# A factorization-machine kernel: one-hot gates from a key in PSUM, picked values kept in PSUM, and a new order for the last jobs

## The chip, the cores and the metric

The kernel runs on one core of one Trainium2 chip. The metric is the device time of one execution in microseconds, the median of several. Engines are named as the profile does: PE is TensorE's matmul side and PEld its weight loads, DVE is VectorE, ACT ScalarE, POOL GpSimd, and SP the engine that issues most transfers.

## The reference

2048 samples, each with 13 dense values and 26 category numbers. Every category field has a table of 12,500 rows of 32 embedding values and one linear value.

```python
sp_emb = emb_tables[fidx, sp_input]          # 2048 x 26 x 32
lin_vals = lin_tables[fidx, sp_input, 0]
lin_output = ds_input @ lin_w.T + lin_b + jnp.sum(lin_vals, axis=1, keepdims=True)
s = jnp.sum(sp_emb, axis=1)
bi_pooled = 0.5 * (s * s - jnp.sum(sp_emb * sp_emb, axis=1))
x = jnp.concatenate([bi_pooled, ds_input], axis=1)
h = jax.nn.relu(x @ w1.T + b1)               # 45 -> 256
h = jax.nn.relu(h @ w2.T + b2)               # 256 -> 128
out = jax.nn.sigmoid(h @ fw.T + fb + lin_output)
```

So the kernel needs, for each sample, the sum and the sum of squares of 26 looked-up rows of 33 values, and then three small layers.

## The kernel before

The lookups are split between two ways of fetching a row.

**19 fields by gather.** The samples form 16 tiles of 128. For each tile, POOL issues 19 indirect DMAs (line 248), one for each field, that bring 128 rows of 33 values into one of three `rows` buffers (`RING = 3`). A tile's first gather waits until the tile three before it has been reduced. DVE sums the rows (`g_sum`, line 314), ACT squares them (line 460), and DVE sums the squares (`g_sq`, line 317).

**7 fields by matmul.** The samples form 4 blocks of 512; a job is one field and one block, 28 jobs in all. A table of 12,500 categories is laid out as 128 partitions x 9 chunks x 11 sub-rows. For each chunk there is a gate, a 128x512 tile with a one where the sample's category lies in this partition and chunk. PE multiplies the chunk's table piece (122 columns for each of three value groups, as a high and a low part) with the gate and adds up over the chunks in `cand`, three PSUM banks of 122x512; two `cand` tiles alternate. This is 9 x 6 = 54 matmuls a job (line 550). The 122 columns hold the 11 possible sub-rows, so DVE's `pick` (line 298) keeps the right one by a compare with the sample's sub-row code and writes it to `picked` in SBUF. DVE adds `picked` to `acc` (line 303), ACT squares `picked` in place (line 455), and DVE adds that to `sq_acc` (line 310).

**The gates.** Three code rows per job come broadcast from DRAM (`codes`). DVE's `make_where` (line 272) makes a mask that holds a chunk value where the partition fits. Three gates are made by DVE from that mask (line 281, two SBUF tensor inputs `where` and `all_one`), six by ACT from it (lines 423, 434, 426). There are 16 gate slots.

**The tables.** A field's table is loaded to `stage` and split by ACT into `high` (line 413) and by DVE into `low` (line 288), in three pieces of three chunks each. `CASTS` says after which job. For the last field, number 6, pieces 0 and 1 are made in iteration 20 and piece 2 in iteration 21, and PE needs piece 2 at chunk 6 of job 22.

**The order.** Each engine has a list of its own. Its main loop runs over j = 0..27. In iteration j, DVE makes the gates of job j+1, picks job j, makes the mask of j+2, casts `low` pieces (`CASTS`), sums a gathered tile (`TILE_AT`: tiles 0 to 11 at the even j from 2 to 24, tiles 12, 13 and 14 at j = 25, 26, 27) and adds the squares. PE runs the 54 matmuls of job j once `cand` is free.

**The end.** Blocks 0, 1 and 2 are complete after jobs 22, 23 and 25, block 3 after job 27. For each block PE folds `acc`, `sq_acc` and the tile sums into two PSUM banks (`fold_block`, lines 554 to 572: sums to `bank_a`, squares to `bank_b`), ACT and DVE form x (lines 469, 470, 325), and PE, ACT run the layers. For blocks 0 to 2 the fold stands after job 23, 24 or 26 and the layers lie between chunks of the next job. Tile 15 arrives last; block 3 is therefore done in two parts, samples 0 to 383 and the last 128. In the prediction E(j) is the moment at which PE ends job j.

## Time and profile before

| | |
|---|---|
| median of 3 runs | 465.53 us (461.74 to 466.88) |
| profiled execution | 466.34 us, its span 464.5 us |
| PE busy | 418.8 us (90%) |
| POOL busy | 357.2 us (77%) |
| DVE busy | 278.0 us (60%) |
| ACT busy | 263.4 us (57%) |

The span runs from the first to the last instruction of the trace; the execution's time is 1.8 us longer. Busy shares are averages over two stages: the jobs up to 20, and the end with folds and layers. PE's busy time is modelled for pipelined matmuls, so 90% does not say how fast they follow one another; the start times do.

### The profile page before, as it was taken

The page shows a single profiled execution, that of the slowest core. Times are in us where ns is not written, and L with a number is a line of the kernel's source. Part 1 is how long each engine was busy: PE and PEld are TensorE (multiplying, and loading weights), DVE is VectorE, ACT ScalarE, POOL GpSimd, SP SyncE. Part 2 cuts the span into 40 slices and gives each one's busy share as a digit, 9 for nine tenths or more (in the row PEclk, how much of TensorE's full clock was granted, in tenths as well). Part 3 has the DMA queues.
Part 4 walks back from the last instruction along what each step waited for, and adds up shares of the span by engine and source line. Part 5 has one row for each costly group of instructions (what it writes and reads, how often), then busy time and mean ns, then how long its engine had stood idle before and what let it go on. Part 6 is the DMA issues. An engine that isn't in the chain of part 4 may idle for free.

```text
span 464.5 us, 4661 instructions
## 1 busy us (share of the span) xinstructions
PE 418.8 (90%) x1700; PEld 302.6 (65%) x1700; DVE 278.0 (60%) x283; ACT 263.4 (57%) x378; POOL 357.2 (77%) x312
## 2 busy tenths in 40 slices
PE   0499999999999999999999999699999999877564
PEld 0377777777777777777777777477564666543122
DVE  6524463687959786878778795776815438122320
ACT  3457776567666776777666676673663717211121
POOL 5777777787878887877777887777877777777770
PEclk9999999999999999999999999889999999959787
DMA  7543336323362326334643325234324222222220
GB/s 208 126 144 50 48 48 185 54 44 45 47 187 28 38 33 192 43 45 48 181 56 47 46 51 184 13 48 46 42 13 47 12 15 11 12 14 14 11 14 3
DMA packets 23600, 28.94 MB, mean 62 GB/s; under 512 B 6245, under 2 KB 22407, under 8 KB 22794
## 3 DMA queue, kind: packets, MB, share of 16 engines
q0 software_dynamic: 9728, 5.16, 19.1%
q1 hardware_dynamic: 13848, 23.49, 17.1%
q8 instruction: 13, 0.21, 0.2%
q14 instruction: 11, 0.08, 0.1%
HBM read 28.53 MB, written 0.09 MB: 62 GB/s over the span
## 4 chain that ended last, share of the span: by engine, by line
POOL 75%; issue 22%; DMA 1%; PE 1%; POOLq 0%; ACT 0%; DVE 0%
POOL rows L248 75%; DMA rows<-table,row_idx 1%; DMA idx_raw<-sparse 1%; PE bank_b L563 0%; POOLq L83 0%; PE bank_a L571 0%; PE cand L587 0%; PE bank_b L571 0%; ACT stage L476 0%; PE cand L580 0%; PE cand L595 0%; DVE g_sum L314 0%; ACT stage L481 0%; DVE xT L325 0%; ACT stage L469 0%
## 5 line engine op out<-in xcount | busy, mean ns | idle before, releaser
L248 POOL DMA_INDIRECT rows<-table,row_idx x304 | 356.4, 1172 | 95.5 <-issue 92.3
L550 PE MATMUL cand<-gates,high 128*122 128x512 f32 x756 | 304.6, 403 | 22.2 <-DVE gates L281 18.2
L550 PE MATMUL cand<-gates,low 128*122 128x512 f32 x756 | 301.3, 399 | 0.0
L550 PEld LDWEIGHTS cand<-gates,high 128*122 128x122 f32 x756 | 140.8, 186 | 68.4 <-DVE gates L281 18.2
L550 PEld LDWEIGHTS cand<-gates,low 128*122 128x122 f32 x756 | 140.6, 186 | 37.4 <-issue 0.7
L455 ACT ACTIVATE picked<-picked 122x1536 f32<-122x1536 f32 x24 | 35.7, 1487 | 96.8 <-DVE acc L303 96.8
L298 DVE SCALAR_TENSOR_TENSOR picked<-codes,sub_id,cand 122x1536 f32<-122x1536 bf16 x24 | 43.5, 1812 | 75.1 <-PE cand L550 75.1
L434 ACT ACTIVATE distance<-where,bias 128x512 bf16<-128x512 bf16 x112 | 71.4, 708 | 6.4 <-DVE where L272 6.2
L426 ACT ACTIVATE gates<-distance,bias 128x512 fp32r<-128x512 bf16 x112 | 71.4, 709 | 0.0
L281 DVE SCALAR_TENSOR_TENSOR gates<-where,all_one 128x512 fp32r<-128x512 bf16 x84 | 53.5, 692 | 0.9 <-ACT sq_acc L452 0.9
L288 DVE TENSOR_TENSOR low<-stage,high 128x1098 fp32r<-128x1098 f32 x21 | 27.2, 1302 | 32.1 <-ACT high L413 32.1
L310 DVE TENSOR_TENSOR sq_acc<-sq_acc,picked 122x1536 f32<-122x1536 f32 x24 | 42.1, 1753 | 4.5 <-ACT picked L455 4.5
L303 DVE TENSOR_TENSOR acc<-acc,picked 122x1536 f32<-122x1536 f32 x24 | 42.4, 1765 | 0.8
L423 ACT ACTIVATE gates<-where,bias 128x512 fp32r<-128x512 bf16 x56 | 37.0, 709 | 0.0
L314 DVE TENSOR_REDUCE g_sum<-rows 128x33 f32<-128x627 f32 (+2 forms) x17 | 21.2, 1249 | 25.3 <-DMA rows<-table,row_idx 25.3
L413 ACT CAST high<-stage 128x1098 fp32r<-128x1098 f32 x21 | 22.9, 1097 | 6.0 <-DMA stage<-tabs 4.2
L272 DVE SCALAR_TENSOR_TENSOR where<-codes,part_id 128x512 bf16<-128x512 bf16 x28 | 20.9, 748 | 5.7 <-DMA codes<-codes_dram 5.7
L460 ACT ACTIVATE squares<-rows 128x608 f32<-128x608 f32 (+2 forms) x17 | 11.5, 674 | 19.6 <-DMA rows<-table,row_idx 19.6
L317 DVE TENSOR_REDUCE g_sq<-squares 128x32 f32<-128x608 f32 (+2 forms) x17 | 20.0, 1175 | 1.5 <-ACT squares L460 1.5
L557 PE MATMUL bank_a<-acc,fold 122*33 122x512 f32 (+2 forms) x30 | 12.9, 572 | 8.7 <-DVE sq_acc L310 8.7
L298 DVE SCALAR_TENSOR_TENSOR acc<-codes,sub_id,cand 122x1536 f32<-122x1536 bf16 x4 | 7.3, 1816 | 20.8 <-PE cand L550 20.8
L452 ACT ACTIVATE sq_acc<-acc 122x1536 f32<-122x1536 f32 x4 | 6.0, 1488 | 15.6 <-DVE acc L298 15.6
(70 smaller groups left out, 102.3 us busy)
## 6 DMA issues: line engine op xcount, KB each, us to landing
codes<-codes_dram SPq DMA_DIRECT2D x28, 384.0 KB, 4.8
stage<-tabs SPq DMA_DIRECT2D x6, 1647.0 KB, 10.1
rows<-table,row_idx POOLq DMA_INDIRECT x304, 3.3
stage<-tabs SPq DMA_DIRECT2D x3, 549.0 KB, 5.4
idx_raw<-sparse SPq DMA_DIRECT2D x1, 208.0 KB, 2.5
w_sb<-w2t SPq DMA_DIRECT2D x1, 128.0 KB
xT<-dense_rows SPq DMA_DIRECT2D x1, 120.0 KB
codes_dram<-col_code SPq DMA_DIRECT2D x1, 84.0 KB
```

The costliest lines, as they stand in the source:

```text
L248: pool.indirect_dma_start(out=rows[t % RING][:, g * W:(g + 1) * W], out_offset=None, in_=table[:, :], in_offset=bass.IndirectOffsetOnAxis( ...
L281: nc.vector.scalar_tensor_tensor(gates[:, g % SLOTS, :], where[j % 2][:, :], float(VALUE[ORDER[k]]), all_one[:, :], ALU.is_equal, ALU.mult ...
L288: nc.vector.tensor_tensor(low[f % 2][:, c, :, :].rearrange("p c q m -> p (c q m)"), stage[:, s], high[f % 2][:, c, :, :].rearrange("p c q ...
L298: nc.vector.scalar_tensor_tensor(into, codes[j % 3][0:M, SUB, :].unsqueeze(1).broadcast_to([M, PARTS, N]), sub_id[0:M, 0:1], cand[j % 2][0 ...
L303: nc.vector.tensor_tensor(acc[:, b, :, :], acc[:, b, :, :], picked[:, :, :], ALU.add).then_inc(summed, 1)
L310: nc.vector.tensor_tensor(sq_acc[:, b, :, :], sq_acc[:, b, :, :], picked[:, :, :], ALU.add).then_inc(sq_summed, 1)
L413: nc.scalar.copy(high[f % 2][:, c, :, :].rearrange("p c q m -> p (c q m)"), stage[:, s]).then_inc(high_made, 1)
L423: nc.scalar.activation(slot, where[j % 2][:, :], ACT.Relu, bias=bias[:, k:k + 1], scale=1.0 if ORDER[DVE_GATES + k] == 8 else -1.0).then_i ...
L426: nc.scalar.activation(slot, distance[:, k - ENDS, :], ACT.Relu, bias=bias[:, ACT_GATES:ACT_GATES + 1], scale=-1.0).then_inc(act_gates, 1)
L434: nc.scalar.activation(distance[:, k, :], where[j % 2][:, :], ACT.Square, bias=bias[:, ENDS + k:ENDS + k + 1]).then_inc(distance_made, 1)
L455: nc.scalar.activation(picked[:, :, :], picked[:, :, :], ACT.Square).then_inc(picked_squared, 1)
L550: last = nc.tensor.matmul(cand[j % 2][0:M, q, :], part[f % 2][:, k, q, :], gates[:, g % SLOTS, :], start=(k == 0 and s == 0), stop=(k == C ...
```

## The change

**Codes.** A sample now has one key per field, chunk x 128 + partition, and the sub-row code; both travel as fp16, so two rows are broadcast in place of three. ACT copies a job's key row into the PSUM bank `bank_a` (`copy_keys`). DVE makes five gates (before: three), each by one `tensor_scalar` that compares `bank_a` with a per-partition number; `where` and `all_one` are gone. ACT makes four gates (before: six) by Square and Relu on the key row in SBUF. There are 18 gate slots, and the gates of job j+2 are made in iteration j (before: j+1).

**Picks.** `pick` writes its result over `cand` in PSUM (the four jobs of field 0 still write `acc`), the two additions read it there, and ACT squares it there. `cand` is therefore released to PE by the addition of squares (`sq_summed`), two jobs ahead, and no longer by the pick.

**Order.** `bank_a` is taken by the keys, so for blocks 0 to 2 the fold of sums, the fold of squares, both halves of layer 1, layer 2 and layer 3 go one after another through `bank_b`. The table `STEPS` puts each after a chunk of jobs 24 to 27.

```diff
-    SLOTS = 16
+    SLOTS = 18
-    DVE_GATES = 3
+    DVE_GATES = 5
-    FOLD_AFTER = {FULL + 3: 0, FULL + 4: 1, FULL + 6: 2}
-    LAYERS_IN = {FULL + 4: 0, FULL + 5: 1, FULL + 7: 2}
+    J0 = FULL + 4
+    STEPS = {(J0, 0): (0, F1), (J0, 4): (0, F2), (J0, 7): (0, L1A), (J0 + 1, 0): (0, L1B), (J0 + 1, 2): (0, L2),
...
+            pool.iota(key_i[:, 0, :], pattern=[[P, CHUNKS]], base=0, channel_multiplier=1).then_inc(made_ids, 1)
+            pool.iota(key_i[:, 1, :], pattern=[[-P, CHUNKS]], base=0, channel_multiplier=-1).then_inc(made_ids, 1)
...
-            def make_where(j):
-
-                dve.wait_ge(codes_in[j % 3], 16 * (j // 3 + 1))
-                if j >= 2:
-                    dve.wait_ge(act_gates, (j - 1) * ACT_GATES)
-                nc.vector.scalar_tensor_tensor(where[j % 2][:, :], codes[j % 3][:, LO, :], part_id[:, 0:1],
-                                               codes[j % 3][:, VAL, :], ALU.is_equal, ALU.mult).then_inc(where_made, 1)
...
-                    nc.vector.scalar_tensor_tensor(gates[:, g % SLOTS, :], where[j % 2][:, :], float(VALUE[ORDER[k]]),
-                                                   all_one[:, :], ALU.is_equal, ALU.mult).then_inc(dve_gates, 1)
+                    nc.vector.tensor_scalar(gates[:, g % SLOTS, :], bank_a[:, :], key_of[:, k:k + 1], None,
+                                            ALU.is_equal).then_inc(dve_gates, 1)
...
-                into = acc[:, b, :, :] if f == 0 else picked[:, :, :]
+                into = acc[:, b, :, :] if f == 0 else cand[j % 2][0:M, :, :]
...
-                    nc.vector.tensor_tensor(acc[:, b, :, :], acc[:, b, :, :], picked[:, :, :],
+                    nc.vector.tensor_tensor(acc[:, b, :, :], acc[:, b, :, :], cand[j % 2][0:M, :, :],
...
-                    nc.vector.tensor_tensor(sq_acc[:, b, :, :], sq_acc[:, b, :, :], picked[:, :, :],
+                    nc.vector.tensor_tensor(sq_acc[:, b, :, :], sq_acc[:, b, :, :], cand[j % 2][0:M, :, :],
...
             for j in range(NJ):
-                if j + 1 < NJ:
-                    make_gates(j + 1)
                 pick(j)
+                if j in (J0 + 1, J0 + 2):
+                    make_x(j - J0)
                 if j + 2 < NJ:
-                    make_where(j + 2)
+                    make_gates(j + 2, 0, 2)
+                add_squares(j)
+                if j + 2 < NJ:
+                    make_gates(j + 2, 2, DVE_GATES)
                 for f, g in CASTS.get(j, ()):
                     low_piece(f, g)
+                if j == J0 - 1:
+                    make_x(0)
                 if j in TILE_AT:
...
+            def copy_keys(j):
+
+                act.wait_ge(codes_in[j % 3], 16 * (j // 3 + 1))
                 if j >= 1:
-                    act.wait_ge(act_gates, j * ACT_GATES)
+                    act.wait_ge(dve_gates, j * DVE_GATES)
+                nc.scalar.copy(bank_a[:, :], codes[j % 3][:, KEY, :]).then_inc(key_copied, 1)
...
+                if j + 2 < NJ:
+                    copy_keys(j + 2)
+                    make_gates(j + 2, 0, FIRST_ACT)
+                if j == J0:
+                    relu1(0, 1)
                 square_picked(j)
...
+                if j + 2 < NJ:
+                    make_gates(j + 2, FIRST_ACT, ACT_GATES)
                 for f, g in CASTS.get(j, ()):
...
+            def fold_sq(m, tiles):
                 b, w = BLOCK[m], COLS[m]
+                if m < BLOCKS:
+
+                    pe.wait_ge(lin_copied, m + 1)
                     pe.wait_ge(y_made, m)
...
             for j in range(NJ):
-                if j >= 2:
-                    pe.wait_ge(cand_free, j - 1)
+                if 2 <= j < BLOCKS + 2:
+                    pe.wait_ge(picked, j - 1)
+                elif j >= BLOCKS + 2:
+
+                    pe.wait_ge(sq_summed, j - 1 - BLOCKS)
```

The instruction order of DVE around the pick of job 20, before (`picked` is the SBUF tile, L288 the `low` pieces, L314 and L317 the tile sums):

```order
L281 SCALAR_TENSOR_TENSOR gates<-where,all_one 128x512 [waits gates_used,where_made]
L281 SCALAR_TENSOR_TENSOR gates<-where,all_one 128x512 [waits gates_used] x2
L298 SCALAR_TENSOR_TENSOR picked<-codes,sub_id,cand 122x1536 [waits sq_summed,gates_used]
L303 TENSOR_TENSOR acc<-acc,picked 122x1536 [waits cand_free]
L272 SCALAR_TENSOR_TENSOR where<-codes,part_id 128x512 [waits act_gates,codes_in1]
L288 TENSOR_TENSOR low<-stage,high 128x1098 [waits high_made] x2
L314 TENSOR_REDUCE g_sum<-rows 128x33 [waits gathered0]
L317 TENSOR_REDUCE g_sq<-squares 128x32 [waits squared]
L310 TENSOR_TENSOR sq_acc<-sq_acc,picked 122x1536 [waits picked_squared]
```

and the same place now:

```order
L293 SCALAR_TENSOR_TENSOR cand<-codes,sub_id,cand 122x1536 [waits gates_used]
L298 TENSOR_TENSOR acc<-acc,cand 122x1536 [waits picked]
L278 TENSOR_SCALAR gates<-bank_a,key_of 128x512 [waits gates_used,key_copied]
L278 TENSOR_SCALAR gates<-bank_a,key_of 128x512 [waits gates_used]
L305 TENSOR_TENSOR sq_acc<-sq_acc,cand 122x1536 [waits picked_squared]
L278 TENSOR_SCALAR gates<-bank_a,key_of 128x512 [waits gates_used,key_copied]
L278 TENSOR_SCALAR gates<-bank_a,key_of 128x512 [waits gates_used] x2
L285 TENSOR_TENSOR low<-stage,high 128x1098 [waits high_made] x2
L309 TENSOR_REDUCE g_sum<-rows 128x33 [waits gathered0]
L312 TENSOR_REDUCE g_sq<-squares 128x32 [waits squared]
```

The gates moved from in front of the pick to behind it, and they now belong to job j+2; the addition of squares moved up, ahead of the casts and the tile sums.

ACT in iteration 21, up to the last `high` piece of field 6, before:

```order
L423 ACTIVATE gates<-where,bias 128x512 [waits gates_used] x2
L426 ACTIVATE gates<-distance,bias 128x512 [waits gates_used,distance_made]
L426 ACTIVATE gates<-distance,bias 128x512 [waits gates_used] x3
L455 ACTIVATE picked<-picked 122x1536 [waits summed]
L413 CAST high<-stage 128x1098
```

and now (L436 squares the pick, L403 is the `high` piece):

```order
L436 ACTIVATE cand<-cand 122x1536 [waits summed]
L418 ACTIVATE distance<-codes,minus_key 128x512 [waits act_gates]
L418 ACTIVATE distance<-codes,minus_key 128x512
L425 ACTIVATE gates<-distance,one 128x512 [waits gates_used,distance_made]
L425 ACTIVATE gates<-distance,one 128x512 [waits gates_used]
L403 CAST high<-stage 128x1098
```

Two distances and two gates of job 23 now stand between the square and the `high` piece, which stood directly behind it.

PE behind the last gate matmul of job 27, before:

```order
L557 MATMUL bank_a<-acc,fold 33x384 [waits sq_summed]
L557 MATMUL bank_a<-acc,fold 33x384 x2
L571 MATMUL bank_a<-ident,g_sum 33x128 [waits reduced]
L571 MATMUL bank_a<-ident,g_sum 33x128 x2
L563 MATMUL bank_b<-sq_acc,fold 32x384 [waits y_made]
```

and now:

```order
L604 MATMUL bank_b<-xT,wl_sb 1x512 [waits h2_made]
L605 MATMUL bank_b<-stage,fw_sb 1x512
L560 MATMUL bank_a<-acc,fold 33x384 [waits summed]
L560 MATMUL bank_a<-acc,fold 33x384 x2
L579 MATMUL bank_a<-ident,g_sum 33x128 [waits reduced]
L579 MATMUL bank_a<-ident,g_sum 33x128 x2
L571 MATMUL bank_b<-sq_acc,fold 32x384 [waits y_made,lin_copied,sq_summed]
```

Layer 3 of block 2 stands behind the job, and the fold of squares of block 3 waits for `lin_copied`, which ACT sets after it has read the folded sums.

## Rows read from the trace of the kernel before

**Rows 1.** The page, chain of work that ended last, shares by engine.

```profile
POOL 75%; issue 22%; DMA 1%; PE 1%; POOLq 0%; ACT 0%; DVE 0%
```

**Rows 2.** One line's instructions (L248): ns min/median/max, first and last start.

```profile
L248 POOL DMA_INDIRECT rows<-table,row_idx x304: 940/944/4380, 4.8 to 452.6; - x152
```

**Rows 3.** Timeline, POOL: start us, us, engine, line, operation [idle before].

```profile
92.69 4.37 POOL L248 DMA_INDIRECT rows<-table,row_idx  x1 [0.30 <-issue]
97.37 0.94 POOL L248 DMA_INDIRECT rows<-table,row_idx  x1 [0.30 <-issue]
98.61 1.96 POOL L248 DMA_INDIRECT rows<-table,row_idx  x1 [0.30 <-issue]
```

**Rows 4.** Timeline, DVE, the same stretch.

```profile
92.67 1.76 DVE L310 TENSOR_TENSOR sq_acc<-sq_acc,picked 122x1536 f32<-122x1536 f32 x1
94.34 1.91 DVE L281 SCALAR_TENSOR_TENSOR gates<-where,all_one 128x512 fp32r<-128x512 bf16 x3
96.15 1.82 DVE L298 SCALAR_TENSOR_TENSOR picked<-codes,sub_id,cand 122x1536 f32<-122x1536 bf16 x1
98.00 1.76 DVE L303 TENSOR_TENSOR acc<-acc,picked 122x1536 f32<-122x1536 f32 x1
```

**Rows 5.** Groups of instructions by form: xcount | busy us, mean ns | idle before.

```profile
L434 ACT ACTIVATE distance<-where,bias 128x512 bf16<-128x512 bf16 x112 | 71.4, 708 | 6.4 <-DVE where L272 6.2
L455 ACT ACTIVATE picked<-picked 122x1536 f32<-122x1536 f32 x24 | 35.7, 1487 | 96.8 <-DVE acc L303 96.8
L288 DVE TENSOR_TENSOR low<-stage,high 128x1098 fp32r<-128x1098 f32 x21 | 27.2, 1302 | 32.1 <-ACT high L413 32.1
L413 ACT CAST high<-stage 128x1098 fp32r<-128x1098 f32 x21 | 22.9, 1097 | 6.0 <-DMA stage<-tabs 4.2 <-DVE sub_id L367 1.9
L314 DVE TENSOR_REDUCE g_sum<-rows 128x33 f32<-128x627 f32 x15 | 19.8, 1321 | 14.9 <-DMA rows<-table,row_idx 14.9
L317 DVE TENSOR_REDUCE g_sq<-squares 128x32 f32<-128x608 f32 x15 | 18.7, 1244 | 1.5 <-ACT squares L460 1.5
L325 DVE TENSOR_TENSOR xT<-stage,bank_b 32x512 f32<-32x512 f32 x3 | 2.0, 670 | 0.6 <-ACT stage L469 0.6
```

**Rows 6.** Waits: us in total, times, longest us.

```profile
DVE g_sum L314 <- DMA rows<-table,row_idx: 25.3, 5, 9.4
```

**Rows 7.** Timeline, DVE, the picks of jobs 16, 20, 23 and 24.

```profile
233.60 1.81 DVE L298 SCALAR_TENSOR_TENSOR picked<-codes,sub_id,cand 122x1536 f32<-122x1536 bf16 x1 [2.97 <-PE cand L550]
283.86 1.81 DVE L298 SCALAR_TENSOR_TENSOR picked<-codes,sub_id,cand 122x1536 f32<-122x1536 bf16 x1 [3.07 <-PE cand L550]
328.22 1.81 DVE L298 SCALAR_TENSOR_TENSOR picked<-codes,sub_id,cand 122x1536 f32<-122x1536 bf16 x1
353.77 1.81 DVE L298 SCALAR_TENSOR_TENSOR picked<-codes,sub_id,cand 122x1536 f32<-122x1536 bf16 x1 [15.54 <-PE cand L550]
```

**Rows 8.** Timeline, PE: the end of a stop, and two passes of layer 1.

```profile
300.31 0.76 PE L550 MATMUL cand<-gates,high 128*122 128x512 f32 x1 [3.99 <-issue]
...
340.81 1.12 PE L580 MATMUL bank_a<-xT,w_sb 48*128 48x512 f32 x2
341.77 1.02 PE L580 MATMUL bank_b<-xT,w_sb 48*128 48x512 f32 x2
```

**Rows 9.** Windows: each engine's busy us (instructions), PEclk, DMA share, GB/s.

```profile
302.00:305.00 3.00, 3.00 (x8) 2.27 (x8) 2.96 (x3) 0.38 (x1) 2.39 (x3) 0.50 0.28 38
```

**Rows 10.** Timeline, the end: DVE, PE, ACT, DVE.

```profile
426.66 1.81 DVE L298 SCALAR_TENSOR_TENSOR picked<-codes,sub_id,cand 122x1536 f32<-122x1536 bf16 x1 [17.00 <-PE cand L550]
435.30 2.13 PE L557 MATMUL bank_a<-acc,fold 122*33 122x384 f32 x3 [8.68 <-DVE sq_acc L310]
450.31 0.48 ACT L487 ACTIVATE y<-cand 1x384 f32<-1x384 f32 x1 [0.99 <-PE cand L595]
455.82 0.38 DVE L314 TENSOR_REDUCE g_sum<-rows 128x33 f32<-128x132 f32 x1 [3.32 <-DMA rows<-table,row_idx]
```

More of the change, by code:

```diff
@@ L142, in build_deep_fm @@
         bank_b = pb("bank_b", [P, N])
-        TAIL = (cand[0][:, 0, :], cand[0][:, 1, :], cand[0][:, 2, :], cand[1][:, 0, :])
-        H1A, H1B, H2P, YP = ([pick] * 3 + [tail] * 2 for pick, tail in zip((bank_a, bank_b, bank_a, bank_b), TAIL))
+        SUM_BANK = [bank_b] * 3 + [bank_a] * 2
+        H1A, H1B, H2P, YP = ([bank_b] * 3 + [cand[k][:, q, :]] * 2 for k, q in ((0, 0), (0, 1), (0, 2), (1, 0)))
         idx_in = sem("idx_in")
@@ L454, in square_picked @@
                     act.wait_ge(summed, j + 1 - BLOCKS)
-                    nc.scalar.activation(picked[:, :, :], picked[:, :, :], ACT.Square).then_inc(picked_squared, 1)
+                    nc.scalar.activation(cand[j % 2][0:M, :, :], cand[j % 2][0:M, :, :], ACT.Square).then_inc(picked_squared, 1)
             def square_rows(t, at, f0, f1):
@@ L517, in _ @@
                     high_piece(f, g)
+                if j == J0:
+                    sigmoid(0)
+                if j == J0 + 1:
+                    relu1(1, 1)
+                    relu2(1)
+                if j == J0 + 2:
+                    relu1(2, 0)
+                    relu1(2, 1)
                 if j in TILE_AT:
@@ L552, in chunk, with fold_sum @@
                 last.then_inc(gates_used, 1)
-            def fold_block(m, tiles):
-                b, w = BLOCK[m], COLS[m]
-                for q in range(PARTS):
-                    nc.tensor.matmul(bank_a[0:W, w], fold[0:M, q, :], acc[:, b, q, w], start=(q == 0), stop=False)
-                pe.wait_ge(reduced, 2 * (tiles[-1] + 1) - 1)
-                fold_tiles(bank_a, g_sum, W, tiles).then_inc(folded, 1)
-                if 1 <= m < BLOCKS:
+            def fold_sum(m, tiles):
+                b, w, bank = BLOCK[m], COLS[m], SUM_BANK[m]
+                for q in range(PARTS):
+                    nc.tensor.matmul(bank[0:W, w], fold[0:M, q, :], acc[:, b, q, w], start=(q == 0), stop=False)
+                pe.wait_ge(reduced, 2 * (tiles[-1] + 1) - 1)
+                fold_tiles(bank, g_sum, W, tiles).then_inc(folded, 1)
+            def fold_sq(m, tiles):
+                b, w = BLOCK[m], COLS[m]
+                if m < BLOCKS:
+                    pe.wait_ge(lin_copied, m + 1)
                     pe.wait_ge(y_made, m)
@@ L573, in fold_tiles, with layer1 @@
                 return last
-            def layer1(m):
+            def layer1(m, k):
                 w = COLS[m]
                 c = slice(BLOCK[m] * N + w.start, BLOCK[m] * N + w.stop)
-                pe.wait_ge(x_made, 2 * m + 2)
-                for k, bank in enumerate((H1A[m], H1B[m])):
-                    nc.tensor.matmul(bank[:, w], w1_sb[:, k * P:(k + 1) * P], xT[:, c], start=True,
-                                     stop=True).then_inc(h1_done, 1)
+                pe.wait_ge(lin_copied, m + 1)
+                pe.wait_ge(x_made, m + 1)
+                if k == 1 and m < BLOCKS - 1:
+                    pe.wait_ge(h1_made, m * HC + 1)
+                nc.tensor.matmul((H1A, H1B)[k][m][:, w], w1_sb[:, k * P:(k + 1) * P], xT[:, c], start=True,
+                                 stop=True).then_inc(h1_done, 1)
             def layer2(m):
```

232 lines of the change are left out of this document (114 added, 118 removed).

## The prediction

> **What bounds the kernel now.** I read the chain of work that ended last first. It is POOL and POOL's own issue time for 97% of the span [rows 1]: nothing released POOL but its previous gather. All 304 gathers run without a break from 4.8 to 452.6 us [rows 2]. Half of them take 0.944 us or less, one takes 4.38. With the 0.30 us in front of each [rows 3], an undisturbed gather is worth 1.245 us, so 304 would last 378.5 us. They last 452.6 + 0.9 - 4.8 = 448.7 us. Some 70 us are prolongations.
>
> The timelines of POOL and DVE beside each other say what prolongs them [rows 3, 4]. The gather at 98.61 ends 1.02 us later than a plain one would; it began while `acc` was being added (98.00 to 99.76). The gather at 92.69 is 3.43 us too long: the addition of squares and three gates follow one another from 92.67 to 96.25. But the gather at 97.37 is a plain 0.94 although it lies within the pick of 96.15 to 97.97. What differs is the operands: the additions, gates and `low` pieces read two SBUF tensors, the pick reads one from SBUF and one from PSUM. So DVE instructions with two SBUF tensor inputs hold gathers up, and one with a PSUM input does not.
>
> PE is the second bound, close behind. Up to job 20 it sets the pace: DVE waits for PE at the picks of jobs 16 and 20, 50.26 us apart, 12.57 us a job [rows 7]. From there on the late gathers stop DVE, five waits with 25.3 us in all [rows 6], and DVE's queue stops PE.
>
> **The change, part by part.**
>
> *Port.* The three large DVE operations and the gates get a PSUM input; the mask goes. Only the 21 `low` pieces of 1.30 us [rows 5] keep two SBUF inputs. They prolong gathers by nothing to 21 x 1.30 = 27 us; I take half, since they would catch a gather at a random point. POOL alone would be through at 4.8 + 378.5 + 14 = 397 us. The bound then passes to PE.
>
> *DVE's load per job.* Pick 1.81 and two additions of 1.76 with one PSUM operand, for which the pick is the nearest row (1.82 against 1.76) [rows 4]: 3 x 1.82 = 5.5. Five gates with PSUM input: nearest above is a 512-wide operation with a PSUM operand, 0.67 [rows 5], below the present gates, 1.91/3 = 0.64 [rows 4]; I take 0.67, 3.3 in all. `Low` pieces three jobs in four (1.0), a tile every second job (2.57/2 = 1.3) [rows 5]. Sum 11.1 of 12.57 us: hidden behind PE with 1.5 us to spare. ACT has 8 gate operations of at most 0.71, the square 1.49, the `high` pieces 0.8 and 0.6 for the keys, under 9 us: hidden too.
>
> *The new wait.* PE may write `cand` again only after pick 1.8, addition 1.8, ACT's square 1.5 and the addition of squares 1.8, 6.9 us after E(j) [rows 4, 5]. PE needs it 12.57 us after E(j), since the other `cand` is in use meanwhile. Cost nothing; the cover is 5.7 us. Queued behind this addition are three gates of job j+2, which PE needs only in the job after next.
>
> *The last table piece.* Here the new order costs. Piece 2 of field 6 is cast in iteration 21 and PE wants it at chunk 6 of job 22, E(21) + 6/9 x 12.57 = 8.4 us. Before, ACT's `high` stood directly behind the square. Iteration 20 on DVE, counted from E(20): pick and addition 3.6, two gates 1.3, the addition of squares until 6.9, three gates until 8.9, two `low` pieces until 11.5, tile sums until 14.0. So the pick of job 21 is 1.4 late. Then on ACT: the square until 6.5, four gate operations until 9.1, `high` until 10.2 and DVE's `low` until 11.5 after E(21). PE stops 3.1 us. In the trace a stop of 3.99 us [rows 8] was followed by a stretch at half clock (0.50, the lower of the two levels; 3 us and 8 matmuls in [rows 9]). Six such microseconds cost 3; I take 1.2 here, between none and 3, as this stop is shorter. Together 4.3 us.
>
> *Folds and layers.* Before, job 24 with one block's fold and layers took 353.77 - 328.22 = 25.6 us, so a block costs 13.0 us of PE [rows 7]. The matmuls are the same, in other places. I followed each wait: x of block 0 stands on DVE in iteration 23 and waits for a fold about 14 us after E(23), but the next pick comes only at 20.7. ACT's Relus find their inputs. Nothing stops PE by more than a few tenths. The three blocks cost 39 us as before, of which layer 3 of block 2 (two passes of 0.96 [rows 8], 1.9) now lies behind job 27.
>
> *Ring.* POOL now waits for its buffers: tile 14 for iteration 24, tile 15 for iteration 25. By the queues this last one is free about 62 us after E(23), at 387, and tile 15 is in `rows` at 414. DVE reaches it at about 425. So the gathers are off the path altogether.
>
> *Start.* The code chain is two operations shorter and a third fewer code bytes travel; ACT's copy of 0.6 replaces the mask. Between nothing and 1 us gained; I take nothing.
>
> *End.* Before, the first part of block 3 took from the last pick, 426.66, to its y at 450.79, 24.1 us [rows 10]. Now PE's fold of sums waits for tile 14's sum only, 8.2 us after the pick (8.64 before [rows 10]); its `acc` passes are done by then; ACT's reading (1.0) lies between the folds in place of 0.5 behind them. From fold to fold's end I get 4.8 us for 7.2, so 20.8 us in all. For the last 128 samples the gathers set the time before: from 455.82 [rows 10] to the end, 464.5, 8.7 us. Now ACT's squares and DVE's sums of tile 15 stand behind y of the first part (1.9 us), then 8.7. Sum from the last pick 31.4 us.
>
> **The sum.** E(20) = 283.8 as before [rows 7]. Jobs 21 to 27: 7 x 12.57 = 88.0. Stop at job 22: 4.3. Folds and layers 39.0, less 1.9 for layer 3 of block 2 and 1.9 for its layer 2, which comes behind chunk 8, so that the pick does not wait for it: 35.2. The last pick starts at 411.3, and with 31.4 the span ends at 442.7. The execution is 1.8 longer than its span: 444.5 against 466.3 profiled. The median shown is 0.8 below the profiled run, which gives **443.5 us**. Its own range is 435 (no stop, the start and additions better) to 453 (a second stop with half clock, DVE 0.2 us a job over its room).
>
> **The rivals.**
>
> *A, the lock stays (0.07).* If gathers are also held up by additions with one SBUF operand, or by the gates' writes, POOL ends near 450 as now and the time is 465.5. Against it: the gather within the pick [rows 3, 4]. For it: no row shows a `tensor_scalar` that reads PSUM. There the Trainium skill, "VectorE: DVE Perf Modes", section "Why PSUM operands drop a tier", says that PSUM has one read port for DVE, so a PSUM operand excludes the mode that takes both SBUF ports; by it this rival falls, and no run here shows it yet.
>
> *B, DVE becomes the bound (0.06), slower.* Three large operations and the gates read PSUM, and the pick and ACT's square write it in place, which no row shows. The PSUM work is 8.8 us a job, the room 1.5. At 1.17 times the price DVE sets the pace; slower than before needs 22 us more, 0.8 a job, so 1.26 times. At 1.3 times it is 28 x (2.6 - 1.5) = 31 us, 474 us. For it speaks that there is little room and no slack in iterations with casts and sums; against it the pick, 0.05 above an SBUF operation. The Trainium skill, "VectorE: DVE Perf Modes", section on the TRN2 errata, gives 120 fixed cycles with a PSUM source against 58 from SBUF; by that estimate each operation costs 0.06 us more, half a microsecond a job, and the sum stays.
>
> *C, PE stops again and again at the end (0.08).* Each of the 17 steps between chunks of jobs 24 to 27 waits for ACT or DVE, whose queues hold gates in front of the Relus. Four stops of about 1.5 us and half clock behind two of them add 12 us: 456. Still faster.
>
> **Chances.** The forecast has 0.79. A measurement of this kernel tells about 1% (4.7 us) from no change. Faster by more: the forecast and C, 0.87. Within 1%: A, 0.07. Slower: B, 0.06. The range of 8 in 10 is 435 to 457; it takes in C and leaves out A and B.
>
> **What would show it.** Gathers of 0.94 us throughout, those at `low` pieces excepted, and POOL with waits for `reduced` behind tile 12. Picks 12.57 us apart with DVE waiting for PE. A stop of PE of about 3 us at chunk 6 of job 22. No DVE wait for gathers. The chain of waits on PE instead of POOL. It is wrong if the additions in PSUM last over 2.1 us, if prolonged gathers remain beside them, or if E(27) - E(23) is above 89 us.

## The result, and the profile after

The changed kernel takes 442.88 us (median of 4 runs, 442.65 to 444.62), the kernel before on the same chip 466.2 (median of 4 runs). The ratio is 0.9538 (95% interval 0.9464 to 0.9613): 4.6% faster. The forecast was 443.5 us in a range of 435 to 457. One of the four runs of the kernel before took 612.89 us; it is left out of the ratio.

That holds for this chip. On another chip the same changed kernel is 17% slower than the kernel before; the experiments below show on what this hangs.

The page of the changed kernel: the shares of busy time, the chain of work that ended last by engine, the costliest groups (count | busy us, mean ns | idle before and what ended it), and the DMA queues (packets, MB, share).

```profile
span 441.3 us, 4680 instructions
PE 410.7 (93%) x1700; PEld 297.4 (67%) x1700; DVE 300.6 (68%) x303; ACT 249.6 (57%) x350; POOL 292.4 (66%) x314
PE 87%; DVE 7%; DMA 3%; ACT 2%; issue 1%; DVEq 0%; ACTq 0%
L253 POOL DMA_INDIRECT rows<-table,row_idx x304 | 291.3, 958 | 116.8 <-issue 90.8
L278 DVE TENSOR_SCALAR gates<-bank_a,key_of 128x512 fp32r<-128x512 f32 x140 | 96.8, 742 | 7.3 <-ACT bank_a L411 6.3
L298 DVE TENSOR_TENSOR acc<-acc,cand 122x1536 f32<-122x1536 f32 x24 | 42.1, 1753 | 0.8
q8 instruction: 13, 0.21, 0.2%
```

The chain is PE's now; before it was POOL's [rows 1]. PE is released by itself at nearly every step.

The gathers answer to [rows 2]: their last start moved from 452.6 to 409.1.

```profile
L253 POOL DMA_INDIRECT rows<-table,row_idx x304: 939/944/1901, 4.9 to 409.1; - x152
```

POOL's timeline while DVE works without a pause, and DVE's beside it. They answer to [rows 3] and [rows 4]; the columns are start, us, engine, line, operation, idle before.

```profile
259.54 0.94 POOL L253 DMA_INDIRECT rows<-table,row_idx  x1 [0.30 <-issue]
...
263.29 0.94 POOL L253 DMA_INDIRECT rows<-table,row_idx  x1 [0.31 <-issue]
```

```profile
257.07 1.82 DVE L293 SCALAR_TENSOR_TENSOR cand<-codes,sub_id,cand 122x1536 f32<-122x1536 f16 x1 [2.42 <-PE cand L553]
258.93 1.75 DVE L298 TENSOR_TENSOR acc<-acc,cand 122x1536 f32<-122x1536 f32 x1
260.60 1.40 DVE L278 TENSOR_SCALAR gates<-bank_a,key_of 128x512 fp32r<-128x512 f32 x2
262.18 1.75 DVE L305 TENSOR_TENSOR sq_acc<-sq_acc,cand 122x1536 f32<-122x1536 f32 x1 [0.18 <-ACT cand L436]
...
282.07 1.82 DVE L293 SCALAR_TENSOR_TENSOR cand<-codes,sub_id,cand 122x1536 f32<-122x1536 f16 x1 [3.69 <-PE cand L553]
295.70 1.82 DVE L293 SCALAR_TENSOR_TENSOR cand<-codes,sub_id,cand 122x1536 f32<-122x1536 f16 x1
304.45 1.29 DVE L285 TENSOR_TENSOR low<-stage,high 128x1098 fp32r<-128x1098 f32 x1
310.36 1.82 DVE L293 SCALAR_TENSOR_TENSOR cand<-codes,sub_id,cand 122x1536 f32<-122x1536 f16 x1 [4.61 <-PE cand L553]
...
410.66 1.82 DVE L293 SCALAR_TENSOR_TENSOR cand<-codes,sub_id,cand 122x1536 f32<-122x1536 f16 x1 [0.47 <-PE cand L553]
```

The gathers at 259.54 and 263.29 start while an addition runs (258.93 and 262.18) and take 0.94 us, as do those beside the pick and the gates. Only 14 of the 304 gathers take more than 0.96 us; 12 of them start beside a `low` piece, which still has two SBUF inputs.

The stop of PE in job 22, against [rows 8], and the granted clock around it, against [rows 9] (PE, PEld, DVE, ACT, POOL busy, PEclk, DMA share, GB/s):

```profile
305.89 0.46 PE L553 MATMUL cand<-gates,high 128*122 128x512 f32 x1 [2.97 <-DVE low L285]
```

```profile
303.00:306.00 3.00, 0.11 (x1) 0.14 (x2) 2.75 (x4) 2.75 (x5) 2.39 (x3) 1.00 0.30 14
306.00:308.00 2.00, 2.00 (x9) 1.61 (x10) 0.00 (x0) 1.65 (x3) 1.51 (x2) 1.00 0.24 21
```

The stop is where the prediction put it, released by `low`, and 2.97 us long. The clock stayed at its higher level (1.00); behind the 3.99 us stop of before it was 0.50.

The longest waits (us in total, times, longest):

```profile
DVE cand L293 <- PE cand L553: 51.5, 15, 7.1
POOL rows L253 <- DVE g_sq L312: 22.9, 5, 13.4
```

There is no wait of DVE for a gathered row, where [rows 6] had 25.3 us; POOL waits for its buffers instead, five times, in front of tiles 11 to 15.

### The profile page after: what moved, and what is told of

It reads as the page before. It is cut to its first block, busy times and chain, and to the rows that moved or that the text cites. A ratio compares the mean times of both kernels' runs of the same rounds, so it can differ in the third digit from the quotient of the medians.

```text
span 441.3 us, 4680 instructions
## 1 busy us (share of the span) xinstructions
PE 410.7 (93%) x1700; PEld 297.4 (67%) x1700; DVE 300.6 (68%) x303; ACT 249.6 (57%) x350; POOL 292.4 (66%) x314
## 4 chain that ended last, share of the span: by engine, by line
PE 87%; DVE 7%; DMA 3%; ACT 2%; issue 1%; DVEq 0%; ACTq 0%
PE cand L553 76%; PE bank_b L571 3%; PE bank_b L560 2%; PE bank_b L579 1%; PE bank_b L590 1%; DMA codes_dram<-col_code 1%; DVE cand L293 1%; DVE acc L298 1%; DVE gates L278 1%; ACT cand L436 1%; DVE low L285 1%; DMA codes<-codes_dram 1%; PE bank_b L597 1%; DVE g_sum L309 1%; DMA idx_raw<-sparse 1%
## 5 line engine op out<-in xcount | busy, mean ns | idle before, releaser
L253 POOL DMA_INDIRECT rows<-table,row_idx x304 | 291.3, 958 | 116.8 <-issue 90.8
L278 DVE TENSOR_SCALAR gates<-bank_a,key_of 128x512 fp32r<-128x512 f32 x140 | 96.8, 742 | 7.3 <-ACT bank_a L411 6.3
L436 ACT ACTIVATE cand<-cand 122x1536 f32<-122x1536 f32 x24 | 34.4, 1435 | 86.3 <-DVE acc L298 86.3
L293 DVE SCALAR_TENSOR_TENSOR cand<-codes,sub_id,cand 122x1536 f32<-122x1536 f16 x24 | 43.7, 1822 | 51.6 <-PE cand L553 51.5
L425 ACT ACTIVATE gates<-distance,one 128x512 fp32r<-128x512 bf16 x112 | 75.1, 716 | 3.1 <-PE cand L553 1.4
L418 ACT ACTIVATE distance<-codes,minus_key 128x512 bf16<-128x512 f16 x112 | 74.1, 711 | 0.1
L305 DVE TENSOR_TENSOR sq_acc<-sq_acc,cand 122x1536 f32<-122x1536 f32 x24 | 42.0, 1752 | 5.3 <-ACT cand L436 5.3
L298 DVE TENSOR_TENSOR acc<-acc,cand 122x1536 f32<-122x1536 f32 x24 | 42.1, 1753 | 0.8
L403 ACT CAST high<-stage 128x1098 fp32r<-128x1098 f32 x21 | 22.9, 1097 | 6.3 <-DMA stage<-tabs 6.3
L411 ACT CAST bank_a<-codes 128x512 f32<-128x512 f16 x28 | 16.3, 583 | 11.7 <-DVE gates L278 6.9
L571 PE MATMUL bank_b<-sq_acc,fold 122*32 122x512 f32 (+2 forms) x30 | 12.9, 574 | 1.1 <-issue 1.1
```

The costliest lines, as they stand in the source:

```text
L253: pool.indirect_dma_start(out=rows[t % RING][:, g * W:(g + 1) * W], out_offset=None, in_=table[:, :], in_offset=bass.IndirectOffsetOnAxis( ...
L278: nc.vector.tensor_scalar(gates[:, g % SLOTS, :], bank_a[:, :], key_of[:, k:k + 1], None, ALU.is_equal).then_inc(dve_gates, 1)
L293: nc.vector.scalar_tensor_tensor(into, codes[j % 3][0:M, SUB, :].unsqueeze(1).broadcast_to([M, PARTS, N]), sub_id[0:M, 0:1], cand[j % 2][0 ...
L298: nc.vector.tensor_tensor(acc[:, b, :, :], acc[:, b, :, :], cand[j % 2][0:M, :, :], ALU.add).then_inc(summed, 1)
L305: nc.vector.tensor_tensor(sq_acc[:, b, :, :], sq_acc[:, b, :, :], cand[j % 2][0:M, :, :], ALU.add).then_inc(sq_summed, 1)
L418: nc.scalar.activation(distance[:, k, :], codes[j % 3][:, KEY, :], ACT.Square, bias=minus_key[:, c:c + 1]).then_inc(distance_made, 1)
```

## The experiments

They ran on four other chips. There the kernel before takes 549 to 566 us by the medians (535 to 590 in single runs) in place of 465, so each run is compared with runs of the kernel before on its own chip, and its numbers stand apart from the result above. Ranges are given where no interval came with a run.

### Additions and gates from SBUF

The first two undo one part of the change each, to see which operands hold gathers. In e1 the picks go back to an SBUF tile:

```diff
+        picks = sb("picks", [M, PARTS, N])
-                into = acc[:, b, :, :] if f == 0 else cand[j % 2][0:M, :, :]
+                into = acc[:, b, :, :] if f == 0 else picks[:, :, :]
-                    nc.vector.tensor_tensor(acc[:, b, :, :], acc[:, b, :, :], cand[j % 2][0:M, :, :],
+                    nc.vector.tensor_tensor(acc[:, b, :, :], acc[:, b, :, :], picks[:, :, :],
...
```

> The changed kernel, but pick writes its result to a tile in SBUF again and both additions and ACT's square work there. Gates, order and PE's waits stay as changed. Theory (a DVE instruction with two SBUF tensor inputs holds gathers up): the 48 additions prolong gathers again, by about 1 us each. POOL's last gather ends near 430 us in place of 410, later gathers stop DVE at tiles 14 and 15, time about 448 us (444 to 455). Rival (the mask and the gates held the gathers up, not the additions): gathers stay at 0.94 us and the time at 443.

Measured: 558.2 us (541.2 to 573.8), before 564.3 (547.6 to 582.9). The groups of e1, and a stretch of its POOL and DVE timelines:

```profile
L254 POOL DMA_INDIRECT rows<-table,row_idx x304 | 333.7, 1098 | 201.6 <-DVE g_sq L315 106.0
L301 DVE TENSOR_TENSOR acc<-acc,picks 122x1536 f32<-122x1536 f32 x24 | 42.2, 1760 | 0.8
```

```profile
150.88 0.94 POOL L254 DMA_INDIRECT rows<-table,row_idx  x1 [16.91 <-DVE g_sq L315]
152.12 2.31 POOL L254 DMA_INDIRECT rows<-table,row_idx  x1 [0.30 <-issue]
154.74 0.94 POOL L254 DMA_INDIRECT rows<-table,row_idx  x1 [0.30 <-issue]
155.99 1.76 POOL L254 DMA_INDIRECT rows<-table,row_idx  x1 [0.30 <-issue]
```

```profile
151.86 1.76 DVE L301 TENSOR_TENSOR acc<-acc,picks 122x1536 f32<-122x1536 f32 x1
153.54 1.41 DVE L279 TENSOR_SCALAR gates<-bank_a,key_of 128x512 fp32r<-128x512 f32 x2
155.18 1.76 DVE L308 TENSOR_TENSOR sq_acc<-sq_acc,picks 122x1536 f32<-122x1536 f32 x1 [0.23 <-ACT picks L439]
```

The gathers that start while an addition runs (152.12 and 155.99) end 0.8 us behind the addition's end; the one that starts beside the gates (154.74) is plain, though an addition begins during it. So what counts is the DVE instruction that runs when a gather starts. All 38 gathers of e1 that start beside one of the 48 additions are prolonged: they take 1.36 to 2.52 us, 1.86 in the mean, or 34.8 us in all over the plain 0.944. The rest of the 42.4 us by which POOL is busier than in the changed kernel (333.7 against 291.3) falls mainly to the `low` pieces: 15 gathers start beside one, 11.4 us over the plain time, where the changed kernel has 3.9. The additions themselves last as long from SBUF (1760 ns) as with a PSUM operand (1753). This part of the mechanism is shown, by the gathers' own durations. Its worth in time is not: the kernel's time on this chip follows something else, as e2 shows. The Trainium skill, "SBUF — State Buffer", section "SBUF: two separate sides", tells of a port pair that DVE and GpSimd lock against each other, for a DVE operation with two SBUF inputs too, though there only against a GpSimd operation that reads SBUF; in the trace the gathers, whose row indices lie in SBUF, are held, by 0.92 us each in the mean (1.86 against 0.94).

e2 keeps the sums in PSUM and reads the keys from SBUF:

```diff
-                    nc.vector.tensor_scalar(gates[:, g % SLOTS, :], bank_a[:, :], key_of[:, k:k + 1], None,
+                    nc.vector.tensor_scalar(gates[:, g % SLOTS, :], keys[:, :], key_of[:, k:k + 1], None,
-                nc.scalar.copy(bank_a[:, :], codes[j % 3][:, KEY, :]).then_inc(key_copied, 1)
+                nc.scalar.copy(keys[:, :], codes[j % 3][:, KEY, :]).then_inc(key_copied, 1)
```

> The changed kernel, but ACT copies the keys to an fp32 tile in SBUF in place of the PSUM bank, and DVE's five gates read it there: one SBUF tensor input each. Theory in its narrow form (only two tensor inputs hold gathers): gathers stay at 0.94 us, gates last 0.64 to 0.74, time 443. Theory in its wide form (an fp32 tensor_scalar from SBUF also takes the second read port, and is faster for it): gates fall to 0.35 to 0.5 us, 140 of them prolong gathers by 0.1 to 0.3 us on average each, POOL's busy time rises by 15 to 40 us, and the time is 443 to 447, since POOL has room.

Measured: 638.1 us (633.0 to 640.4), ratio to before 1.1354 (1.1139 to 1.157).

```profile
L254 POOL DMA_INDIRECT rows<-table,row_idx x304 | 297.6, 979 | 289.7 <-DVE g_sq L313 196.1
L279 DVE TENSOR_SCALAR gates<-keys,key_of 128x512 fp32r<-128x512 f32 x140 | 61.1, 487 | 10.1 <-issue 7.5
```

A gather that is held, and the gates beside it:

```profile
268.38 1.24 POOL L254 DMA_INDIRECT rows<-table,row_idx  x1 [0.30 <-issue]
268.23 1.27 DVE L279 TENSOR_SCALAR gates<-keys,key_of 128x512 fp32r<-128x512 f32 x3
```

A gate from SBUF takes 487 ns in place of 742. These gates hold gathers too. Of the 23 gathers that start beside one, 20 take more than 0.96 us; the mean is 1.12 and the longest 1.29 us, and in the median they end 0.82 us behind that gate, just as gathers do behind an addition. Beside the gates from PSUM, 83 gathers of the changed kernel start and none is prolonged. The price is small, 4.0 us of POOL's 297.6, because the gates are short and few gathers meet one, not because they leave gathers free; the `low` pieces add 5.0 us here. The wide form of the expectation came true in its two mechanisms (0.35 to 0.5 us a gate, 0.1 to 0.3 us a gather), and missed the time. The Trainium skill, "VectorE: DVE Perf Modes", section "Why PSUM operands drop a tier", says that a PSUM operand shuts out the mode with both read ports; 742 against 487 ns agrees.

Against expectation was the time. e1, whose gathers are held up, is 80 us faster than e2, whose gathers are nearly free. Something in free gathers costs time on this chip. A window of e1, 160 us long (PE, PEld, DVE, ACT and POOL busy us with instructions, PEclk, DMA share, GB/s), has PE at its full rate with the gathers 1.5 us apart:

```profile
160.00:320.00 160.00, 156.65 (x670) 121.87 (x668) 128.86 (x118) 101.26 (x139) 127.53 (x107) 1.00 0.35 63
```

### Fewer gathers

Both kernels with 15 gathers a tile in place of 19 (four gathered fields are left out of the sums). The edit of e4, and with the old names of e3:

```diff
+    SKIP = 4
-                for g in range(GF):
+                for g in range(SKIP, GF):
-                    dve.wait_ge(gathered[t % RING], (t // RING + 1) * 16 * GF)
-                    sum_rows(t, t, 0, GF)
+                    dve.wait_ge(gathered[t % RING], (t // RING + 1) * 16 * (GF - SKIP))
+                    sum_rows(t, t, SKIP, GF)
...
```

> The kernel before with 15 gathers a tile in place of 19 (four of the 19 gathered fields are left out of the sums). Theory (all of the gain came from POOL's gathers leaving the path): POOL needs 449 x 15/19 = 354 us, is off the path, and the old kernel ends on PE: last pick at about 284 + 88 + 39 = 411 us, then 24 us to y of the first part and 10 for the last 128 samples, time about 447 us (443 to 451). Rival (the new gates and the new order of folds and layers gave part of it): 453 us or more.

> The changed kernel with 15 gathers a tile in place of 19 (the same four fields are left out). Theory (gathers are off the path now): 442 to 443 us, nothing gained beyond about 0.5 us of shorter sums. Rival (ring waits and late tiles still cost at the end): 438 us or less.

Measured: e3, the kernel before with 15, 476.5 us, ratio 0.8478 (0.8347 to 0.861). e4, the changed kernel with 15, 550.0 us, ratio 0.9765 (0.9419 to 1.0112). So the kernel before gains 88 us from 64 gathers fewer, more than their own 64 x 1.25 = 80, and the changed kernel, which on the first chip was bound by PE, is not bound by it here: it is 73 us behind e3. Both expectations were missed (447 and 442 to 443 us), so how much of the 4.6% came from the gathers and how much from the new gates and order was not measured.

The same two on the next chip, with their edits unchanged:

> The kernel before with 15 gathers a tile in place of 19 (four gathered fields are left out of the sums), once more, since all runs beside the first one, the kernel before included, were disturbed. Theory (all of the gain came from the gathers leaving the path): 447 us (443 to 451). Rival (the new gates and order gave part of it): 453 us or more.

> The changed kernel with 15 gathers a tile in place of 19 (the same four fields are left out), once more for the same reason. Theory (gathers are off the path): 442 to 443 us. Rival (ring waits still cost): 438 us or less.

Measured: e9 474.5 us (472.9 to 475.6), e10 522.0 (520.4 to 531.3), before 548.6 (535.0 to 564.8). The order is the same: it is no accident of one chip. Both expectations were missed again.

### The casts of the last piece, and block 3 in one part

These were meant to shorten the stop of 2.97 us and the end. e5 casts the last piece directly behind the square and the addition of squares:

```diff
+                if j == FULL + 1:
+                    low_piece(MMF - 1, 2)
-                for f, g in CASTS.get(j, ()):
+                for f, g in CASTS.get(j, ()) if j != FULL + 1 else ():
...
```

> The changed kernel, but in iteration 21 ACT makes piece 2 of field 6's high part directly behind the square of the pick, and DVE its low part directly behind the addition of squares, both ahead of the last gates. Theory (PE's stop of 2.97 us at chunk 6 of job 22 comes from that order alone): the low piece is ready 2.1 to 2.7 us earlier, the stop falls to 0.3 to 0.9 us, every later start moves up by as much, and the time is 440.5 us (439.5 to 441.5). Rival (the stop gives room to queues that are late anyway, and the time comes back at the steps of jobs 24 to 27): 442.5 to 443.

e8 does that as well, sums tiles 11 to 15 in iterations 23 to 26 and takes block 3 whole:

```diff
-    TILE_AT[25], TILE_AT[26], TILE_AT[27] = 12, 13, 14
+    del TILE_AT[24]
+    TILE_AT[23] = 11
-    COLS = [slice(0, N)] * 3 + [slice(0, N - P), slice(N - P, N)]
-    BLOCK = [0, 1, 2, 3, 3]
+    COLS = [slice(0, N)] * 4
+    BLOCK = [0, 1, 2, 3]
...
```

> As the last one, and block 3 is done in one piece of 512 samples: tiles 11 to 15 are summed at places where DVE and ACT were waiting for PE in iterations 23 to 26, all before the pick of job 27, and the layers run once. Theory (gathers are off the path, and the split of block 3 is now only a second serial chain): from the last pick to the end 19 to 20 us in place of 30.6, time about 429 us (427 to 433). Rival (tile 15 lands too late for it, since its buffer comes free late): DVE waits for it before the last pick, 435 us or more.

Measured: e5 647.9 us (645.0 to 653.0), e8 646.4 (641.2 to 648.7), before 548.6. Both are some 100 us slower than the kernel before, and a few us between them can't be read beside that. For their purpose these runs are inconclusive. e11 is e8's kernel once more, with no other variant beside it:

> The kernel with the last cast first and block 3 in one piece, once more, alone beside the kernel before. In the eight runs so far PE stood still for instructions that came one in 1.4 us, in stretches of 20 to 40 us, which the profiles of the kernel before and of the change do not show. Theory of the change (gathers off the path, the split only a second serial chain): without such stretches 429 us (427 to 433), 19 to 20 us from the last pick to the end. Rival (tile 15 lands too late): 435 us or more. If the stretches are there again they belong to the chip or to this kernel and not to the company of other kernels, and the time is near 646.

Measured: 647.8 us (640.5 to 658.9), ratio 1.1695 (1.1534 to 1.1857). The other variants don't matter.

### The changed kernel itself on another chip

No edit:

> The changed kernel as it is, on another chip. In the nine runs of variants PE got one instruction in 1.4 us wherever POOL's gathers ran at 7 to 8 in 10 us, and ran at its full 43 matmuls in 10 us as soon as POOL paused for a buffer. Theory (on such a chip undisturbed gathers starve PE of instructions, and the locks of the kernel before were a brake that kept gathers apart): the changed kernel takes about 640 us where the kernel before takes 555, although it gained 5% on the first chip. Rival (the stretches come from what the variants changed): the changed kernel is faster than the kernel before here too, by about 5%.

Measured: 636.1 us (628.0 to 639.8), before 552.0 (544.1 to 562.7), ratio 1.1657 (1.1543 to 1.1772). The same code that was 4.6% faster is 17% slower. Windows of 10 us of e13, with the same columns:

```profile
50.00:60.00 10.00, 2.34 (x4) 1.11 (x4) 1.96 (x2) 3.89 (x6) 7.87 (x8) 0.50 0.25 13
...
90.00:100.00 10.00, 10.00 (x45) 7.87 (x44) 4.84 (x7) 8.25 (x11) 0.00 (x0) 0.99 0.10 27
...
160.00:170.00 10.00, 10.00 (x44) 7.87 (x43) 9.78 (x11) 8.14 (x12) 7.56 (x9) 1.00 0.34 40
...
190.00:200.00 10.00, 2.29 (x4) 1.09 (x4) 0.00 (x0) 0.00 (x0) 7.56 (x9) 0.50 0.26 13
```

and the same kernel's on the first chip:

```profile
50.00:60.00 10.00, 10.00 (x45) 7.88 (x45) 4.35 (x4) 5.82 (x8) 7.55 (x8) 1.00 0.28 17
```

With POOL gathering at full rate PE issues 4 matmuls in the 10 us from 50 and from 190 on; while POOL stands still (from 90) it issues 45. On the first chip it issues 45 beside the same gathers. DMA share (0.25 against 0.28) and GB/s (13 against 17) are no higher than there, so it is not the amount of data. DVE and ACT run nothing from 190 to 200, so it is not their work in PSUM either.

Dense gathers alone are not enough, though: from 160 to 170 POOL has its 9 gathers and PE its 44 matmuls, on the same chip. The gathers of e13 form 13 unbroken stretches. In eleven of them the starts of PE's instructions fall to 1.40 us apart. The first such step comes 14 to 33 us after the stretch began, the last within 4 us of its last gather; the stretch from 153 to 201 us, for one, has its first at 171.7. So what PE bears badly is a long run of dense gathers, not each of them.

The timeline of such a stretch, all engines:

```profile
61.31 0.58 PE L553 MATMUL cand<-gates,low 128*122 128x512 f32 x1 [1.51 <-issue]
62.10 0.95 POOL L253 DMA_INDIRECT rows<-table,row_idx  x1 [0.30 <-issue]
62.71 0.28 PEld L553 LDWEIGHTS cand<-gates,high 128*122 128x122 f32 x1 [1.82 <-issue]
63.35 0.94 POOL L253 DMA_INDIRECT rows<-table,row_idx  x1 [0.30 <-issue]
64.11 0.58 PE L553 MATMUL cand<-gates,high 128*122 128x512 f32 x1 [2.21 <-issue]
64.60 0.95 POOL L253 DMA_INDIRECT rows<-table,row_idx  x1 [0.30 <-issue]
65.51 0.28 PEld L553 LDWEIGHTS cand<-gates,low 128*122 128x122 f32 x1 [2.52 <-issue]
```

One PE instruction starts every 1.40 us, weight load and matmul in turn. Nothing that the profile shows holds it ("issue"). The waits and DMA queues of e13:

```profile
POOL rows L253 <- DVE g_sq L312: 198.2, 11, 34.0
PE cand L553 <- issue: 132.4, 79, 17.4
```

```profile
q8 instruction: 13, 0.21, 0.2%
```

PE crawls, so DVE and ACT get no work, so tiles aren't reduced, and POOL waits 198 us for buffers; in these pauses PE catches up. The packets that load instructions are as many as on the first chip and have the same share (0.2%); 13 of them in the whole run can't space single instructions 1.40 us apart, which speaks against the loading of code.

A rival stands untested: that the recording of the trace holds PE. Every execution in this document, here and on the first chip, has a span and a granted clock, and so was a recorded one. A gather raises its semaphore in 16 steps, 4,864 for the 304 gathers. The first chip's trace of the changed kernel has 4,861 of them; e13's has 1,083, and those of the other runs on these four chips 949 to 1,853 (3,840 would be all with 15 gathers a tile). So profiles from these chips can't give the time from issue to landing of a gather, which stands behind x304 on the first chip (first line) and is missing in e13:

```profile
rows<-table,row_idx POOLq DMA_INDIRECT x304, 3.2
rows<-table,row_idx POOLq DMA_INDIRECT x304
```

The recorder may suffer from the same thing as PE, be its cause, or have nothing to do with it. No run without a record shows which.

### Gathers paced and spaced

If dense gathers starve PE, thinning them out must free it, with nothing else changed. e12 is e8's kernel, in which each gather first waits until PE has used so many gates:

```diff
+                    n = t * GF + g
+                    due = int(0.947 * n - 19) if n <= 209 else int(179 + 0.564 * (n - 209))
+                    if due > 0:
+                        pool.wait_ge(gates_used, due)
```

> The kernel with block 3 in one piece, and each of POOL's gathers also waits until PE has used a number of gates (0.947 per gather less 19 up to gather 209, 0.564 behind it), so that POOL can't run ahead of a PE that has fallen behind. Without starvation these waits cost about nothing, since the buffers already hold POOL to that pace. Theory (gathers starve PE, and a PE that is behind must be given pauses): time falls from 647 to 520 or less, with POOL pausing between single gathers. Rival (PE's supply fails by itself, and POOL merely runs meanwhile): 640 to 650, since PE would crawl with gathers paused too.

Measured: 529.7 us (524.3 to 536.2), before 552.0 (544.1 to 562.7) on the same chip. The same kernel without pacing took 646 and 648 on two other chips, the changed kernel 636 on this one. The 520 us that were expected at most were missed by 10 us, and the rival (640 to 650) is out: against that kernel the gathers' timing alone was changed, so gathers do hold PE up here. A window of e12, 40 us long:

```profile
40.00:80.00 40.00, 33.92 (x129) 25.19 (x129) 21.37 (x23) 23.75 (x32) 24.42 (x26) 0.87 0.30 32
```

and of e11, the same kernel unpaced:

```profile
40.00:80.00 40.00, 8.49 (x15) 3.89 (x14) 0.00 (x0) 0.72 (x1) 28.29 (x30) 0.50 0.26 13
```

In the same 40 us there are 129 matmuls beside 26 gathers, against 15 beside 30. PE's idle time at "issue" is 57.8 us in e12 against 132.4 in e13.

e14 is the changed kernel with a small POOL operation before each gather:

```diff
+        rest = sb("rest", [P, 64])
+        rested = sem("rested")
+                    pool.memset(rest[:, :], 0.0).then_inc(rested, 1)
+                    pool.wait_ge(rested, t * GF + g + 1)
```

> The changed kernel, but POOL sets a small tile to zero in front of each gather and waits for that, so that gathers start about 1.5 us apart in place of 1.25, or 6 to 7 in 10 us. The variant with sums in SBUF showed PE at its full 43 matmuls in 10 us for 130 us on end at that rate, and starved at 8. Theory (only dense gathers starve PE): PE is not starved, POOL is the bound again, 304 x 1.5 = 456 us, and on a chip where the changed kernel takes 636 and the kernel before 552 this one takes 475 to 495. On a chip like the first it takes the same 475. Rival (the rate is not what matters but the number of gathers or the stretch without a pause): it starves too, 540 or more.

Measured: 533.9 us (513.1 to 557.6), before 565.7 (554.4 to 572.3). Its windows:

```profile
50.00:60.00 10.00, 6.25 (x21) 3.51 (x20) 5.20 (x6) 4.53 (x7) 8.10 (x15) 0.95 0.37 40
...
100.00:110.00 10.00, 10.00 (x45) 7.90 (x44) 4.65 (x4) 2.48 (x3) 8.10 (x16) 1.00 0.40 91
```

(Half of POOL's instructions are the memset.) The gathers are 1.39 us apart where I had meant 1.5; PE issues 21 matmuls in 10 us in place of 4, and 45 at other times. The expected 475 to 495 us were missed by 39 us and more, and the rival's "540 or more" was missed too; the direction was right. 0.14 us between gathers is worth some 100 us, against e13's 636 on another chip, and against the 648 us of e11, which has another end, on this one. That PE still falls to 21 matmuls fits e13: spacing the gathers without a pause lessens the hold-up and does not end it.

## Why the prediction was right, and where its terms were off

*The port.* Right. Gathers are 0.94 us beside PSUM additions, picks and gates, and 1.86 us in the mean beside SBUF additions (e1). The prediction took the gather at 97.37 as lying within the pick; it ends at 98.31, behind the start of an addition, and is plain because it had started before. The rule of two SBUF inputs was too narrow: a gate with one SBUF tensor input holds gathers as well (e2). The remainder was estimated at 14 us from 21 `low` pieces; POOL's busy time gives 304 x (0.958 - 0.944) = 4 us. It was off the path.

*DVE's load.* The additions last 1.75 where 1.82 was taken, the gates start 0.66 to 0.69 us apart in a row (three in 2.06), where 0.67 was taken. DVE waits for PE 2.42 + 3.69 us in the four jobs up to the pick at 282.07, 1.5 us a job, the room that was worked out. Rival B did not come: PSUM operands cost nothing extra. Rival A fell with the port. Of rival C, PE's repeated stops, only the stop of job 22 was there.

*Start and pace.* E(20) was taken as 283.8 from [rows 7] and is 282.07: 0.9 us from an earlier first gate matmul (17.32 against 18.24), the rest from 12.50 us a job in the mean for 12.57. "Between nothing and 1 us" was the bound of the start, and its other end was the true one.

*The stop.* Predicted 3.1 us and released by `low`; measured 2.97. The term of 1.2 us for the clock behind it was wrong: the clock stayed at 1.00.

*Folds and layers.* From the pick of job 20 to that of job 27 it took 128.59 us; 88.0 + 4.3 + 35.2 = 127.5 were predicted. With the 1.2 us of the clock gone, jobs, folds and layers took 2.3 us more than the rows gave. It lies in jobs 24 to 27: from the pick of job 23 (322.83) to that of job 27 it took 87.8 us, of which folds and layers are 87.8 - 4 x 12.5 = 37.8 in place of 35.2. PE is busy for all of that stretch, at a clock of 1.00, so it is not rival C's stops; the steps themselves, at 17 places between the chunks, cost those 2.6 us, and the jobs being 0.07 us shorter each gives a little back. Which of the steps cost it was not tried.

*The ring.* POOL's waits for buffers began in front of tile 11, where they were expected behind tile 12. They cost nothing: the last gather started at 409.1, and DVE summed tile 15 from 425.7 on.

*The end.* From the last pick at 410.66 to the end at 441.3: 30.6 us, predicted 31.4. Its two parts missed in opposite directions: y of the first part came 21.7 us behind the pick (predicted 20.8), the last 128 samples took 9.0 more (predicted 1.9 + 8.7 = 10.6).

So the sum is right to 1.4 us of span (442.7 against 441.3), and by nearly the terms it names: the largest misses are -1.7, -1.2, +2.3 and -0.8, and they cancel in part; that much of the close hit is luck. (The last step of the sum gives 444.5 - 0.8 = 443.7, not 443.5.) What the prediction did not contain is that free gathers can harm PE. Its argument took gather and matmul as independent, since the trace of before showed PE's pace at 12.57 us a job beside gathers; on the first chip that is true at 8 gathers in 10 us too. On the other chips I tried it is not. There the hold-ups that the change removes probably acted as a brake that kept the gathers thin: e1, which puts them back, takes 558 us, the level of before, where e2, with its sums in PSUM, takes 638 on the same chip. There is no trace of the kernel before itself on these chips; its variant with 15 gathers, e9, has the slow steps once, up to 65 us (6 matmuls beside 9 gathers from 50 to 60), and hardly again.

*What stays open.* Why the first chip is free of this. Its own run of 612.89 us for the kernel before may be the same thing; it has no trace. By what path gathers hold PE's instructions up was not found, nor why it takes a long stretch of them; the amount of data is excluded by the rows above, code loading is unlikely, and the recording of the trace stands as a rival. The changes of e5 and e8 have no price.

## What to carry to other kernels

- A hold-up that a change removes may have been a brake. Ask what the freed engine will run into at full rate, even where the two share no data, and give that case a chance of its own.
- Where gathers aren't the bound, let them follow the consumer's progress: each waits for so many gates used. Here it gave 18% (530 us against 647 of the same kernel without, on other chips; the changed kernel takes 636 on the same chip), and it was not tried on the chip that did not need it.
- A verdict from one chip holds for that chip. Time the kernel before and after on a second one before keeping a change of this kind.

## What the runs showed of the hardware

- On four chips of five, PE falls to one instruction in 1.40 us in the later part of long stretches of indirect gathers 1.25 us apart, and in e13 it is free within 4 us of their end. e13 has 4 matmuls beside 9 gathers in the 10 us from 190 on, and 44 beside 9 from 160 on. Gathers 1.39 us apart left 21 matmuls in the 10 us from 50 on, against 4 (e13) and 45 (first chip). The matmuls of such stretches run at the lower clock level (0.50). All of this was seen in recorded executions, whose traces lack most landing events on these chips.
- A DVE addition with two SBUF inputs holds a gather that starts beside it until 0.82 us behind its own end (median of 38 gathers in e1; 1.86 us in the mean in place of 0.94). An fp32 `tensor_scalar` from SBUF does the same (e2: 20 of 23 gathers, 1.12 us in the mean); from PSUM it holds none of 83, and takes 742 ns in place of 487.
- A stop of PE of 2.97 us left the clock at 1.00; one of 3.99 us, in the kernel before, was followed by 0.50.
